# Landing waits on GpSimd behind every third gather of a two-layer graph kernel

## The reference

```python
# layer 0: rows of source nodes and of edges, summed by target
agg_h = jax.ops.segment_sum(feat_n[src], dst, num_segments=N)
agg_e = jax.ops.segment_sum(edge_feat, dst, num_segments=N)
rst = jnp.concatenate([agg_h, agg_e], axis=1) @ weight

# layer 1: the same edges, weighted
messages = edge_val[:, None] * embeddings[edge_src]
neighbor_emb = jax.ops.segment_sum(messages, edge_dst, num_segments=embeddings.shape[0])
```

## Time and profile before

| what | before |
| --- | --- |
| time, median of 3 runs | 2390.53 us (2380.89 to 2390.94) |
| the profiled execution: its span | 2408.5 us |
| POOL busy | 908.1 us (38%) |
| PE busy | 1864.4 us (77%) |
| DVE busy | 1245.5 us (52%) |
| ACT busy | 705.9 us (29%) |
| gathers of line 650: count, busy, mean | 638, 623.8 us, 978 ns |

### The profile page before, as it was taken

One profiled execution on the slowest core, in us unless ns is written; L12 is line 12 of the kernel. 1 busy time (PEld: TensorE's weight loads), 2 busy tenths in 40 slices (PEclk: granted clock), 3 DMA queues, 4 the chain that ended last, 5 costly groups with the idle time before them and its releaser, 6 DMA issues. The chain is left out here.

```text
span 2408.5 us, 34947 instructions
## 1 busy us (share of the span) xinstructions
PE 1864.4 (77%) x10583; PEld 1445.5 (60%) x10584; DVE 1245.5 (52%) x3264; ACT 705.9 (29%) x1624; POOL 908.1 (38%) x933
## 2 busy tenths in 40 slices
PE   6598568667385999999936876558889884699975
PEld 4365346445263999999923454335566572588875
DVE  6553676667474444444474644542344376433345
ACT  5122333333431111111156710111222132133324
POOL 0555464656120222222203245446566200245442
PEclk9999688889696999999977988768899997699997
DMA  7454443444353111101143133223333226312124
GB/s 231 133 136 127 116 118 98 125 119 123 124 218 116 33 32 33 32 32 33 30 134 102 37 105 90 71 84 98 97 115 112 63 75 255 142 61 64 63 57 146
DMA packets 171237, 239.46 MB, mean 99 GB/s; under 512 B 74146, under 2 KB 139262, under 8 KB 168693
## 3 DMA queue, kind: packets, MB, share of 16 engines
q0 software_dynamic: 42336, 112.74, 16.7%
q1 hardware_dynamic: 116884, 113.45, 14.4%
q10 hardware_dynamic: 11904, 11.96, 1.6%
HBM read 184.86 MB, written 56.12 MB: 100 GB/s over the span
## 5 line engine op out<-in xcount | busy, mean ns | idle before, releaser
L650 POOL DMA_INDIRECT agg_message<-table,edges_src x638 | 623.8, 978 | 641.6 <-PE agg_partial L713 205.4
L2817 PEld LDWEIGHTS ex_p_h<-ex_xT,ex_own_up 128*128 128x128 f32 (+1 forms) x2464 | 281.4, 192 | 2.7 <-issue 1.3
L2817 PE MATMUL ex_p_h<-ex_xT,ex_own_up 128*128 128x128 f32 (+1 forms) x2464 | 282.1, 276 | 1.0 <-DVE ex_xT L2868 1.0
L2872 DVE COPY ex_own_up<-moe_up 128x1280 f32 x114 | 100.5, 882 | 168.8 <-PE ex_p_h L2817 168.0
L2776 POOL DMA_INDIRECT ex_x<-moe_in,route_token_at x58 | 57.3, 988 | 312.1 <-PE ex_p_x L2807 242.3
L709 PE MATMUL agg_partial<-agg_message,moe_up 128*64 128x321 f32 x638 | 115.0, 487 | 47.9 <-issue 14.1
L2860 ACT ACTIVATE ex_gate_h<-ex_p_h 128x640 f32<-128x640 f32 x56 | 39.5, 705 | 315.3 <-PE ex_p_h L2817 315.3
L3013 ACT COPY ex_own_up<-moe_up 128x1024 f32 x66 | 67.5, 1044 | 215.4 <-PE ex_p_h L2986 169.8
L2942 POOL DMA_INDIRECT ex_x<-moe_in,route_token_at x66 | 64.4, 975 | 169.7 <-PE ex_p_x L2973 87.3
L2986 PEld LDWEIGHTS ex_p_h<-ex_xT,ex_own_up 128*128 128x128 f32 x1024 | 118.8, 195 | 12.4 <-issue 10.6
L2986 PE MATMUL ex_p_h<-ex_xT,ex_own_up 128*128 128x128 f32 x1024 | 123.4, 280 | 3.4 <-issue 1.2
(11 more groups left out here) (665 smaller groups left out, 3701.0 us busy)
## 6 DMA issues: line engine op xcount, KB each, us to landing
moe_up<-in_f_w SPq DMA_DIRECT2D x8, 1386.0 KB
agg_message<-in_edge_rows SPq DMA_DIRECT2D x54, 192.0 KB
agg_message<-table,edges_src POOLq DMA_INDIRECT x638
sums<-agg_span SPq DMA_DIRECT2D x107, 80.2 KB
moe_up<-in_f_w SPq DMA_DIRECT2D x4, 2048.0 KB, 14.6
moe_down<-in_f_w SPq DMA_DIRECT2D x4, 2048.0 KB
sums<-agg_span SPq DMA_DIRECT2D x107, 64.0 KB
moe0b_down<-in_f_w SPq DMA_DIRECT2D x8, 768.0 KB
```

What stands on the lines that cost most here:

```text
L650: pool.indirect_dma_start(out=to[:, k * w:k * w + D], out_offset=None, in_=self.table, in_offset=bass.IndirectOffsetOnAxis(ap=self.edges.s ...
L2817: return pe.matmul(to, own_up[:, o:o + n], xT[:, k * D + c * P:k * D + (c + 1) * P], start=(c == 0), stop=(c == 1))
L2872: dve.tensor_copy(own_up[:, a:b], at(up, e * U0 + a, b - a)).then_inc(up_copied, 1)
```

## The change

In `gather`, a helper `landed` is added that makes POOL wait until the first n gathers of a group have landed. It is used twice: ahead of a group's first gather, for all gathers of the group before, and ahead of its fourth gather (`n == RUN`), for its first three. The wait for `used` stays where it was.

```diff
+    def landed(self, pool, g, n):
+        pool.wait_ge(self.gathered[g % self.ring], (g // self.ring * GE + n) * 16)
+
     def gather(self, pool, g):
         if g >= self.ring:
             pool.wait_ge(self.used, g - self.ring + 1)
         to, w = self.slot(self.message, g, self.width), self.width
-        for k in self.tiles(g):
+        if g:
+            self.landed(pool, g - 1, len(self.tiles(g - 1)))
+        for n, k in enumerate(self.tiles(g)):
+            if n == RUN:
+                self.landed(pool, g, n)
             t = self.place(g) + k
             pool.indirect_dma_start(out=to[:, k * w:k * w + D], out_offset=None, in_=self.table,
```

## The result

The changed kernel takes 2528.3 us (median of 4 runs, 2525.1 to 2529.3) against 2388.1 us (4 runs, 2380.9 to 2390.9) beside it: 1.0589 times as long, with a 95% interval of 1.0565 to 1.0613, or 140 us more. The forecast was 2494 us, +103 us, with a range of 2425 to 2565. So the sign and the range hold, and a quarter of the loss is not in the sum. The profiled execution of after took 2528.8 us, its span is 2526.7 us, and it stands at its median; that of before stood 18 us above its own.

The account below looks back on a forecast made before the run. POOL waited for PE before; with the waits POOL would bound the mixer and feed-forward. 63.6 us (channels and mixer) plus 40.5 (feed-forward) gave +104, scaled to 103, on 2390.5: 2494 us, range 2425 to 2565.

Parts of the forecast that it names:

- the price of a wait: POOL's wait for its own gather's landing, twice per group, taken as 2.3 us, making a group 11.5 us instead of 7.5.
- The quiet bound: Lower limit for one wait, 1.84 us, from a gather in the expert stage that released PE with no other DMA traffic.
- Channels +18.3: Channels stage: its end passes from DVE to POOL, and the mixer's first gather starts 18.3 us later.
- Mixer +45.3: Mixer: 36 groups at 11.5 us put the landing of group 52 63.6 us later, the channels stage's 18.3 included.
- Feed-forward +40.5: Feed-forward: 30 groups at 11.5 us from 1609.49 end at 1954.5 against 1914.04, +40.5 us.
- the pace at which PE uses groups up: PE's use of gathered groups: 10.24 us each in the mixer, 10.15 in the feed-forward; POOL had 2.2 to 2.7 us spare.
- keys: nothing: Layer 1's keys: groups 0 to 3 gathered by 1342.3, before PE's first product at 1354.61; no cost.
- attention: nothing: Layer 1's attention: POOL, held by PE, would issue groups 21 and 22 by 1597.7, ahead of 1609.49; no cost, 11 us cover.
- The first: Rival: waits up to 1.63 us keep a group under PE's pace, 2390 us; chance 0.05 together with the fourth.
- the fourth: Rival: landings already past at the head, only the middle wait counts, 9.5 us a group, 2390 us; 0.05 with the first.
- The second: Rival: the queue empties and every landing is the quiet one, 2419 us; chance 0.12 for 2403 to 2440.
- The third: Rival: landings meet other DMA traffic, waits of 2.84 us, 2583 us; chance 0.11 for above 2560.

Follow-up runs that it names:

- swapped kernel: Changed kernel with the wait for `used` moved behind the landing wait at a group's head: 2477.9 us, ratio 1.0392 to the kernel before.
- second profile: The kernel before, unedited, run and profiled a second time: 2389.2 us, span 2387.1 us.
- the two kernels with the gap ahead of the fourth gather: Changed kernel without head wait, six tiny POOL writes replacing the middle wait: 2346.5 us; the same with middle landing waits in layer two's first four groups: 2311.3 us.

## Why the prediction was right in sign and short in size

**The mechanism of the loss held.** With both waits POOL becomes the bound in the mixer and the feed-forward, the ring doesn't help, and each tenth of a us in the wait is multiplied by the groups. POOL waits for PE no more there, and PE waits for gathers; the trace puts that down to "issue" (5.57 us ahead of the product at 712.23), not to the DMA, but the last gather of that group ends at 709.38 + 0.94 = 710.32, 1.91 us before the product.

**The term that was mis-sized is the price of a wait.** 2.3 us were taken; 178.9 / 72 = 2.48 us were measured in the mixer. The quiet bound of 1.84 us came from PE; POOL, told of its own gather, starts 2.05 to 2.09 us behind the end of the issue at best, so the lower end was too low by 0.2 us for this engine. The Trainium skill, "DMA: Bandwidth & Descriptors", section "Anatomy of one DMA — SWDGE (gpsimd) path", gives the estimate of 2.3 us for 128 KB that the prediction worked out; counted from the end of the issue, the swapped kernel's 2.06 to 2.19 us lie just under it, so the trace agrees with that reading and not with the one from the start. At the head some 0.4 us more come from the second wait, which no row of before could show as an instruction of its own; it was not asked for in the sum.

**Step by step.** Group 0 at no cost: right, group 1 starts at 81.78 instead of 81.58. Channels +18.3: measured +34.2, since a group takes 12.5 us there (81.78 to 269.99 for 15). Mixer +45.3 beyond that: +62.0, at 12.0 us a group. Feed-forward +40.5: +53.8. These three are the wait's price again; together they are 46 us over the sum, and 53 us against the second profile of the kernel before.

**The steps that failed** are "the pace at which PE uses groups up" and, with it, "keys: nothing" and "attention: nothing". The prediction read 10.24 us a group off two starts and took it for TensorE's own work. With one gather in place of six it is 7.44 us. The pace of before is that of engines held up by the gathers themselves, and a wait that spaces the gathers lifts part of it: 22 to 25 us in the keys and up to 8 in the attention. That gave back 33 of the 46 us by the first profile and 21 of the 53 by the second, whose span stands at the median: 104 + 53 - 21 is 136 of the 140 us measured. The step "11 us of cover" in the attention is wrong too: POOL bounds that stage from start to end in the changed kernel, at 12.0 us a group (the heads of groups 6 and 22 at 1469.71 and 1661.72), and the stage is no longer for it than in the second profile of before.

**The rivals.** The first and the fourth were "a wait under PE's pace costs nothing, 2390 us". That case was run, with the middle wait alone: POOL's group is 9.7 us as rival 4 worked it out (9.5), and the time is not 2390 but 2313. The second, quiet landings throughout, had 2419 us: with the waits swapped the medians in the mixer are 2.16 us at the head and 2.09 in the middle, near POOL's quiet 2.05, and the time is still 2478; its sum had 1.84 for the quiet wait. The third put a dear wait down to traffic, 2583 us. Of the 0.43 us by which 2.48 lies above the quiet 2.05, some 0.3 go with the order of two waits and 50 us with them; how much of the rest is traffic was not tried. "Faster, for which no row shows a way" was a row not asked for: the earlier trace rows have PE busy in 261 of 369 us of the mixer, and the list of waits has ScalarE's 82.8 us with no releaser beside it. What the second wait costs on top of the first is 2528 - 2313 = 215 us; the change as a whole is that loss less the 73 us that its other half gains.

**What stays open.** It is shown that TensorE's raises come late where gathers follow closely, that outside the keys' stage the bytes have no part in it, and that gathers 1.70 us apart end it with POOL waiting for no landing. Why the keys' stage stands still at 1.40 us a gather and hardly at 1.55 is not shown: 128 row addresses, 16 raises and POOL's issuing were never varied apart. Nor is it shown whether a raise is late or the end of the work behind it, since the ends of products are modelled, nor why the two kernels with the gap ahead of the fourth gather are 2 and 3% faster with late raises of 446 and 429 us. One suspect can be weighed: the Trainium skill, "SBUF — State Buffer", section "Who interferes with whom", tells of a port that VectorE and GpSimd share, where one fully blocks the other. L819 reads two inputs, so it was a candidate. But it starts 0.02 us behind the raise that it waits for, so no port held it up in between, and ScalarE, which the same page gives ports of its own, waits as well, at 1302.32 for TensorE alone.

## What to carry to other kernels

A pace read off two starts is what a stage does, not what its busiest engine could do: before taking it for a bound, add up what that engine waits for, and ask for idle time that ends with no releaser in the record. A wait for a landing costs its round trip times the waits on the path as soon as its engine is the bound, and can be worth something as a brake below that; try half of it before judging the whole. Where one wait instruction has to stand alone, let it be the one that is answered early.

## What the runs showed of the hardware

- POOL, waiting for its own gather of 128 rows of 1 KB, goes on 2.05 to 2.09 us behind the end of the issue in quiet stretches; with a second semaphore to wait for, written so that the landing's stands on its own instruction, 2.54 us.
- While POOL issues a gather every 1.25 us, raises of TensorE come up to 11.2 us late (112 of 232 in the kernel before by more than 0.3 us), those of VectorE and ScalarE don't (0 of 32 and 0 of 155). With 1.70 us between gathers the late ones come to 7 us instead of 392 to 454. Outside the keys' stage the bytes moved make no difference (ratio 0.9975 for an eighth).
- Such a stop costs twice, since the granted clock falls while TensorE stands idle. The kernel before, second profile, three windows of 3 us, first ahead of the stop, then in it and behind it (the clock is the third number from the end):

```profile
1298.00:1301.00 3.00, 2.59 (x17) 1.59 (x15) 0.01 (x1) 2.28 (x7) 2.24 (x3) 1.00 0.37 116
...
1310.00:1313.00 3.00, 0.00 (x0) 0.00 (x0) 0.00 (x0) 0.00 (x0) 2.39 (x3) 0.50 0.40 108
...
1325.00:1328.00 3.00, 3.00 (x6) 1.06 (x5) 1.70 (x6) 3.00 (x10) 0.00 (x0) 0.50 0.00 0
```

It goes from 2.4 to 1.2 GHz, and the four products of L1752 behind the stop take 3.78 us instead of 1.98:

```profile
1302.74 1.98 PE L1752 MATMUL kv_p_kv<-layer_kw,layer_XNT 128*128 128x512 f32 x4 [2.15 <-issue]
...
1323.93 3.78 PE L1752 MATMUL kv_p_kv<-layer_kw,layer_XNT 128*128 128x512 f32 x4 [3.55 <-ACT layer_XNT L1691]
```

In the mixer the mean is 0.83 in the kernel before, 0.88 with the middle wait and 0.93 with one gather a group.
